# Causal attention in four stages on one core: the turning of the second maxima and the value projection moved behind the second row sums and the first products

## The reference, cut to what matters

```python
x = x + attention(layernorm(x), Wq, Wkv, Wo, bo)
...
s = einsum('bhid,bhjd->bhij', q * Dh**-0.5, k)          # 16 heads of 64, 1024 x 1024 a head
gm = max(s, axis=-1, keepdims=True)
p = where(causal_mask, 0.0, exp(s - gm))                # the maximum is over the full row, the sum is causal
out = einsum('bhij,bhjd->bhid', p, v) / (sum(p, axis=-1, keepdims=True) + 1e-8)
return out.transpose(...).reshape(B, N, H * Dh) @ Wo + bo
```

## Time and profile before

| | us |
|---|---|
| median of 3 runs (1958.75 to 1962.0) | 1960.1 |
| the profiled execution, its own time | 1959.38 |
| its span, first to last instruction | 1957.7 |
| PE busy over the span | 1804.2 (92%) |
| DVE busy | 1454.0 (74%) |
| POOL busy | 1312.8 (67%) |
| ACT busy | 1006.7 (51%) |
| mean granted clock of PE | 0.956 of full speed |

### The profile page before, as it was taken

How to read it: one execution, slowest core, us unless ns; L and a number is a source line. 1 busy time by engine, 2 the same in 40 slices (tenths; PEclk the granted TensorE clock), 3 DMA queues, 4 the chain that set the end, 5 groups by cost and what they waited for, 6 DMA issues and landing times. The chain is left out here.

```text
span 1957.7 us, 32851 instructions
## 1 busy us (share of the span) xinstructions
PE 1804.2 (92%) x11830; PEld 1277.6 (65%) x11830; DVE 1454.0 (74%) x2497; ACT 1006.7 (51%) x2066; POOL 1312.8 (67%) x1327
## 2 busy tenths in 40 slices
PE   6999999999999999999999999959999478849998
PEld 4666666666666666666666666648777255538886
DVE  7777777777787777786877777649889156777998
ACT  3544444445345444444444444437888555436776
POOL 1777677667676676676756766838889245517998
PEclk9999999999999999999999999979999588968999
DMA  2000000000000000000000000000000000000000
GB/s 88 2 1 1 2 1 1 1 1 1 1 2 1 1 1 2 1 1 1 1 1 1 1 1 1 22 22 1 1 1 1 7 1 1 1 0 7 12 12 17
DMA packets 15089, 10.89 MB, mean 6 GB/s; under 512 B 433, under 2 KB 14546, under 8 KB 14930
## 3 DMA queue, kind: packets, MB, share of 16 engines
q1 hardware_dynamic: 14930, 8.80, 1.6%
HBM read 6.70 MB, written 2.10 MB: 4 GB/s over the span
## 5 line engine op out<-in xcount | busy, mean ns | idle before, releaser
L1217 DVE TENSOR_REDUCE attn_neg<-attn_shared 128x2 f32<-128x1024 f32 x512 | 618.6, 1224 | 289.1 <-PE attn_shared L1350 287.7
L1100 ACT ACTIVATE attn_prob<-attn_shared 128x1024 f32<-128x1024 f32 (+3 forms) x384 | 311.1, 812 | 460.4 <-PE attn_shared L1378 393.3
L1012 POOL TENSOR_TENSOR attn_row_sum<-attn_row_sum,attn_prob 128x1024 f32<-128x1024 f32 (+3 forms) x256 | 417.0, 1629 | 24.2
L497 ACT ACTIVATE experts_weighed<-experts_y,kept_gate 128x128 f32<-128x128 f32 x1024 | 278.2, 402 | 69.1 <-PE experts_y L724 54.4
L1007 POOL TENSOR_TENSOR attn_row_sum<-attn_prob 128x1024 f32<-128x1024 f32 x64 | 135.7, 2120 | 236.2 <-ACT attn_prob L1100 233.6
L580 DVE SCALAR_TENSOR_TENSOR experts_acc<-experts_y,kept_gate,experts_acc 128x128 f32<-128x128 f32 x960 | 262.4, 340 | 21.1 <-PE experts_y L724 19.1
L989 POOL TENSOR_TENSOR attn_prob<-attn_prob,attn_below 128x256 f32<-128x256 f32 x256 | 188.3, 736 | 79.2 <-ACT attn_prob L1100 75.6
L1346 PE MATMUL attn_shared<-attn_qk_hi 64*128 64x512 f32 x1024 | 224.8, 426 | 4.2 <-DVE attn_qk_lo L1230 2.4
L1236 DVE RECIPROCAL attn_den<-attn_den 128x256 f32<-128x256 f32 x128 | 214.7, 1719 | 13.3 <-ACT attn_den L1124 13.3
L1350 PE MATMUL attn_shared<-attn_qk_hi,attn_qk_lo 64*128 64x512 f32 x1024 | 209.3, 392 | 0.0
L1348 PE MATMUL attn_shared<-attn_qk_lo,attn_qk_hi 64*128 64x512 f32 x1024 | 208.5, 391 | 0.0
(11 more groups left out here) (227 smaller groups left out, 3256.1 us busy)
## 6 DMA issues: line engine op xcount, KB each, us to landing
kept_x<-in_L_attn_a_x_dram SPq DMA_DIRECT2D x4, 512.0 KB, 8.7
out_dram<-kept_x SPq DMA_DIRECT2D x8, 256.0 KB, 2.3
attn_prob<-in_L_attn_a_Wkv_dram SPq DMA_DIRECT2D x2, 512.0 KB, 6.3
kept_half_raw<-_ffn_expert_weights_dram SPq DMA_DIRECT2D x2, 512.0 KB, 4.5
last_other_half<-_ffn_expert_weights_dram SPq DMA_DIRECT2D x2, 512.0 KB, 5.2
attn_prob<-in_L_attn_a_Wq_dram SPq DMA_DIRECT2D x1, 512.0 KB, 4.8
attn_wo<-in_L_attn_a_Wo_dram SPq DMA_DIRECT2D x1, 512.0 KB, 5.7
attn_bo<-in_L_attn_a_bo_dram SPq DMA_DIRECT2D x1, 64.0 KB, 5.7
```

The source lines that it names most:

```text
L497: ins = act.activation(weighed[n][:, e, :], y[fill(pair, quad, odd) % RING][:, e * D:(e + 1) * D], ACT.Copy, scale=k.gate[:, c, quad * PER ...
L1012: pool.tensor_tensor(row_sum[n][:, :, at:], row_sum[n][:, :, at:], src[:, :, at:], ALU.add).then_inc(add_ok, 1)
L1100: act.activation(prob[n % RING][:, :, at:], buffer((p, i))[:, :, at:], ACT.Exp).then_inc(exp_ok, 1)
L1217: dve.tensor_reduce(neg[p % 2][:, :, b, half], buffer((p, b, half))[:, :, :], AX.X, ALU.max, negate=True).then_inc(max_ok, 1)
```

## The change

The lists of PE and ACT in the middle of each round are reordered, and the list `single` with them. No operation is added or removed.

```diff
         if out_group(r) is not None:
             shared.append(("out", out_group(r), 0))
+        if valid(r - 1):
+            single.append(("sum", r - 1, 1))
         if valid(r):
             single.append(("turned", r, 1))
-        if valid(r - 1):
-            single.append(("sum", r - 1, 1))
         if valid(r + 1):
             single.append(("turned", r + 1, 0))
@@ ACT
                         if valid(r - 1):
                             product_out(r - 1, 1)
+                            denominator(r - 1, 1)
                         if valid(r):
                             rows(r, 1)
                         for u in value_units(r, 0):
                             values(*u)
                         if job_at(r, 3) is not None:
                             turned_high(job_at(r, 3))
-                        if valid(r - 1):
-                            denominator(r - 1, 1)
@@ PE
                 if valid(r - 1):
                     for i in range(8, 12):
                         product(r - 1, i)
+                if valid(r - 1):
+                    sums(r - 1, 1)
+                if valid(r):
+                    for i in range(0, 3):
+                        product(r, i)
                 if valid(r):
                     turned(r, 1)
                 for u in value_units(r, 0):
                     values(*u)
                 if job_at(r, 3) is not None:
                     turn_batch(job_at(r, 3))
-                if valid(r - 1):
-                    sums(r - 1, 1)
-                if valid(r):
-                    for i in range(0, 3):
-                        product(r, i)
 
                 row_stage(r, 1)
```

## The result

| | before | after |
|---|---|---|
| median of the runs, us | 1959.73 (4 runs) | 1979.47 (4 runs, 1977.34 to 1984.15) |
| ratio, 95% interval | | 1.0102 (1.009 to 1.0114) |
| span of the profiled execution, us | 1957.7 | 1977.3 |

The account below looks back on a forecast made before the run. PE's own list was taken to bound attention (busy 1163.44 of 1175.00 us at full clock). The terms -0.2 + 3.7 + 5.5 + 8.4 - 0.9 = +16.5 us gave a median of 1976.5, range 1968 to 1981.

Parts of the forecast that it names:

- Plain rounds: Eleven rounds without norming work, and round 0: values run into a row stage, saving 0.02 us each, -0.2 in all.
- Step 2: Six rounds with half a norming on ACT before product_out: PE idles before the products, losing 0.62 us each, 3.7 in all.
- Step 1: Six rounds with ACT's square root: products late, 0.62 us; table load late, 0.29; 0.91 each, 5.5 in all.
- rival 3: The long table switch: ACT's switch costs the exponential another 1.38 us; 1984.8 us, chance 0.04.
- Step 3: Six rounds in which a batch is turned: s1 waits for turned_low, st7 late; loss 1.40 us each, 8.4 in all.
- Rounds 30 and 31: Rounds without values: sums' wait for rows goes, -0.9 us in round 30; nothing put for round 31, bound -0.9.
- 1 (cheaper neighbours): Rival: fewer switches between kinds of matmul save 6.0 us instead of 0.2 over some thirty rounds; 1970.7 us, chance 0.16.
- 2 (won back): Rival: slack in row stages or at the round's end takes up the late starts, only gains stand; 1953.2 us, chance 0.04.
- 4 and 5: Rivals: 4, new waits all hidden, 1960 us, chance 0.04; 5, late maxima double step 3's 1.4, 1985 us, chance 0.04.

Follow-up runs that it names:

- e12: Changed kernel with the turning moved behind the values and the batch, directly ahead of the second row stage; 1977.3 us.
- e4: Changed kernel with one 128x1 exponential on ACT behind the denominator in square-root rounds, so the exponentials' table loads there; 1979.6 us.
- e2: Changed kernel with the old order in the six rounds in which a batch is turned; 1970.9 us.

## Why the prediction was right, and where it was short

**Plain rounds: right.** -0.02 each was forecast, +0.02 measured. That it came so near is luck in part. Two small terms were missed that cancel: 0.06 less in the middle and 0.08 more in the stage. The prediction called the value copy hidden by 0.08 because it asked when s1's matmul is due, 2.88 behind the first value matmul; the weight load ahead of it is due at about 2.77 (1.60 to s0, and 1.17 more as in the kernel before), the copy ended at 2.73, and PE took 0.12 and not 0.07 to go on. And s1 late did cost something: s1 then ended late, and with it the second maximum, for which st8 waits (e12).

**Step 2: right in kind, 0.80 where 0.62 was forecast.** The term for the new edges was mis-sized: PE starts the product 0.10 behind the copy and not 0.07, the second products take 2.73 to the turning and not 2.67, and the stage grew by the same 0.09 as in plain rounds.

**Step 1: 1.03 where 0.91 was forecast**, by the same edges. The stage grew by 0.32 where 0.29 was forecast, but of that the table load is 0.24, which e4 took away, and 0.08 is the growth of the plain rounds. s2 came 3.19 behind s0 where 3.09 was forecast. On the drain the trace decides: the exponentials start at 578.81, 0.01 behind the end of the load at 578.80, with PE waiting for the first of them. The Trainium skill's 1.38 us of drain beside each load (ScalarE: Activation LUTs, section What ACT_TABLE_LOAD costs) is not seen here, and rival 3 falls.

**Step 3: 1.32 where 1.40 was forecast.** s1 came 2.58 behind s0 (2.50 forecast) and st7 3.62 (3.70 forecast), and the rest of the stage carried it on to its end (+1.38), as the prediction had it; the middle is 0.06 shorter, which it had not. e2 gave it back.

**Rounds 30 and 31.** Round 30 gained 0.77 where 0.94 was forecast (0.9 in the sum): the turning to s0 costs 0.59 and not 0.41, an edge that no row of before showed. Round 31's gain of 0.80 in the middle was taken back at the end: the last sixteen products, the later ones of which wait for POOL's masks (L989), took 5.04 us to the sums where they took 4.23. Zero was right, for the reason that the prediction gave.

**Rivals.** 1 (cheaper neighbours): no, values to s0 stayed at 1.60, and s0's first pair at 0.50. 2 (won back): no, nothing was recovered. 4 and 5: no. The forecast's 16.5 fell 1.8 short of the 18.3 that the rounds show: 1.1 in step 2, 0.7 in step 1, 0.4 in plain rounds and 0.1 in round 30 short, and 0.5 too much in step 3. Of the last 1.4 us up to 19.7, 0.1 is round 0, 0.6 the start and 0.4 the stretch behind attention; what made these two longer no run shows, and the rest is within the scatter of the runs. The sizes that were missed mostly lay on one side, so 1979.5 came near the upper end of the range.

## What to carry to other kernels

Here one engine was nearly always busy, moving its parts about gained less than 0.1 us a round by itself, and each part was also the cover of some other engine's latency. Before moving one, list for each kind of round who reads the buffer in front of it and how long the shortest time to the next user becomes; in this kernel the eighteen rounds with extra work made the loss, and the plain ones showed next to none. And put all the copies that the bound engine waits for ahead of work that can wait, not one of them: the same edit gained 12 us in one order and lost 6 in the other, until the second copy went with the first.

## What the runs showed of the hardware that was not expected

- A matmul whose output buffer comes free just in time still pays about 0.1 us: its weight load started 0.03 us ahead of it and not 0.11 or 0.12 (e12), and the first pair showed 0.50 us and not 0.39. The Trainium skill (TensorE: Matmul & The Clock Gate, section Step-by-step: what each phase is for) says that PE pulls weight loads ahead of matmuls in flight; the trace of e12 agrees for s1, with 0.11 us.
- An activation table switch cost 1.28 us and 0.01 to 0.02 to the next activation, in both directions; for the exponentials PE was waiting at the time.
- The distance from one kind of matmul to the next depends on the pair: turning to values 0.41 us, turning to a row stage 0.59; products to turning 2.31 and to sums 2.21 for the same 16 matmuls.
